# Both score passes as fp32r products of high and low parts, maxima turned on TensorE, elementwise work shared out anew

## The reference

```python
# _ref: q = layernorm(x) in 16 heads of 16, k = v = ctx
scores = jnp.einsum('bhqd,bhkd->bhqk', q, k) * scale
scores = jnp.where(causal_mask, scores, jnp.finfo(scores.dtype).min)
out = jnp.einsum('bhqk,bhkd->bhqd', jax.nn.softmax(scores, axis=-1), v)
# FFN
prob = jax.nn.softmax(xf @ w_router + b_router, axis=-1)
_, idx = jax.lax.top_k(prob, TOP_K)                 # mask: 1 for the 4 blocks in idx
h = jax.nn.relu(jnp.einsum('nd,ebd->neb', xf, w1b) + b1b[None])
y = jnp.einsum('neb,ebd,ne->nd', h, w2b, mask) + b2
# whole
x = x + jnp.tanh(g_xattn[0]) * xattn(layernorm(x), ctx, ctx)
x = x + jnp.tanh(g_ffn[0]) * ffn(layernorm(x), ...)
```

## Time and profile before

| | |
|---|---|
| time, median of 3 runs | 773.07 us (771.96 to 773.37) |
| profiled execution | 772.89 us, of which the span of the trace is 771.1 us |
| granted TensorE clock, mean | 0.987 of full |
| busy TensorE / its weight loads | 728.8 / 676.5 us (95% / 88%) |
| busy VectorE, ScalarE, GpSimd | 577.0, 432.7, 486.7 us |
| DMA, mean | 38 GB/s |

### The profile page before, as it was taken

One profiled execution on the slowest core, in us unless ns is written; L12 is line 12 of the kernel. 1 busy time (PEld: TensorE's weight loads), 2 busy tenths in 40 slices (PEclk: granted clock), 3 DMA queues, 4 the chain that ended last, 5 costly groups with the idle time before them and its releaser, 6 DMA issues. The chain is left out here.

```text
span 771.1 us, 26802 instructions
## 1 busy us (share of the span) xinstructions
PE 728.8 (95%) x11496; PEld 676.5 (88%) x11496; DVE 577.0 (75%) x1362; ACT 432.7 (56%) x780; POOL 486.7 (63%) x663
## 2 busy tenths in 40 slices
PE   4578899999999999999999999999999999999877
PEld 3457799999999999999999999999999999998877
DVE  5278787778778877787887778778777877877652
ACT  2266556655665565566556555655665566556432
POOL 5386566667666766676676667666766766665432
PEclk9599999999999999999999999999999999999999
DMA  6201111111011111101111110111111101000000
GB/s 161 67 31 31 29 45 34 40 44 32 29 43 45 43 30 44 44 16 44 43 44 30 44 43 20 41 44 44 41 33 45 35 25 43 17 16 2 16 28 28
DMA packets 30101, 29.65 MB, mean 38 GB/s; under 512 B 3745, under 2 KB 29473, under 8 KB 29985
## 3 DMA queue, kind: packets, MB, share of 16 engines
q1 hardware_dynamic: 29984, 27.95, 11.8%
HBM read 19.03 MB, written 8.39 MB: 36 GB/s over the span
## 5 line engine op out<-in xcount | busy, mean ns | idle before, releaser
L661 POOL TENSOR_SCALAR_AFFINE_SELECT weights<-weights 128x1024 f32<-128x1024 f32 x128 | 137.6, 1099 | 130.6 <-ACT weights L434 130.6
L668 POOL TENSOR_TENSOR h_low<-hid,h_high 128x512 fp32r<-128x512 f32 x128 | 166.1, 1297 | 56.2 <-ACT hid L456 55.3
L567 DVE SCALAR_TENSOR_TENSOR hid<-bank,b_cols,used_all 128x256 f32<-128x256 f32 x256 | 111.2, 475 | 72.2 <-PE bank L362 63.9
L360 PE MATMUL bank<-xT_high,w_high 128*128 128x256 f32 x512 | 154.7, 302 | 3.6 <-DVE hid L567 3.6
L514 DVE TENSOR_REDUCE q_pad<-score_banks 128x16 f32<-128x2048 f32 x64 | 146.0, 2282 | 9.5 <-PE score_banks L258 9.5
L434 ACT ACTIVATE weights<-score_banks 128x1024 f32<-128x1024 f32 x128 | 124.3, 1024 | 43.1 <-PE score_banks L274 43.1
L378 PE MATMUL bank<-w_high,h_high 128*128 128x256 f32 x512 | 143.7, 281 | 2.6 <-DVE y_out L552 2.6
L361 PE MATMUL bank<-xT_low,w_high 128*128 128x256 f32 x512 | 144.4, 282 | 0.0
L362 PE MATMUL bank<-xT_high,w_low 128*128 128x256 f32 x512 | 144.1, 282 | 0.0
L379 PE MATMUL bank<-w_low,h_high 128*128 128x256 f32 x512 | 143.0, 279 | 0.0
L380 PE MATMUL bank<-w_high,h_low 128*128 128x256 f32 x512 | 143.0, 279 | 0.0
(11 more groups left out here) (76 smaller groups left out, 1286.3 us busy)
## 6 DMA issues: line engine op xcount, KB each, us to landing
c_in<-in_ctx SPq DMA_DIRECT2D x32, 256.0 KB, 2.8
x_in<-in_x SPq DMA_DIRECT2D x32, 256.0 KB, 3.1
out_y<-y_out SPq DMA_DIRECT2D x32, 256.0 KB, 2.2
w_stage<-in_w1T SPq DMA_DIRECT2D x1, 1024.0 KB, 8.8
hid<-in_w2T SPq DMA_DIRECT2D x16, 64.0 KB
qT<-qT SPq DMA_DIRECT2D x64, 8.0 KB
b_cols<-in_b SPq DMA_DIRECT2D x16, 0.2 KB
b_all<-in_b SPq DMA_DIRECT2D x1, 128.0 KB, 4.1
```

The source lines that it names most:

```text
L360: pe.matmul(out=bank, lhsT=w1_high[:, k, c], rhs=high, start=k == 0, stop=False)
L567: dve.scalar_tensor_tensor(hid[:, n % 4, j], banks[HID_BANK][:, j * TOKS:(j + 1) * TOKS], b1_cols[:, c:c + 1], used_all[:, p % 2], ALU.add ...
L661: pool.affine_select(out=w, in_=w, compare_op=ALU.is_ge, fill=0.0, base=0, pattern=[[0, 2 * HB], [1, S]], channel_multiplier=-1).then_inc( ...
L668: pool.tensor_tensor(h_low[:, p % 2, chunks], hid[:, n % 4], h_high[:, p % 2, chunks].bitcast(F32), ALU.subtract).then_inc(h_low_made, 1)
```

## The change

- Queries and context are split in a high part, rounded to fp32r, and a low part. For the context both lie side by side in the 32 columns of a head (`c_parts`) before they are turned; for the queries each value stands twice (`qn`), and the split is made after the transpose: ScalarE's copy rounds (`qT_high`), VectorE subtracts (`queries_low`). A product of 32 rows then holds (q high or low) x (k high + k low). Both passes run over `qT_high` and `qT_low`.
- The maximum goes through `neg_max` in a high and a low part, is turned by TensorE by itself (`max_transposed`), copied by ScalarE (`max_evacuated`), and is added in the second pass by four more products per 128 columns with the constant `pick`. `max_row` and its 64 DMAs go, `MAX_LAG` goes.
- The sum of x and attention goes from VectorE to GpSimd, the gate is multiplied into the normalisation. The two reciprocal roots of a turn are made in one pair of instructions (`deviations`).
- Hidden units: ScalarE adds the bias and clips from PSUM, in four instructions of 256 a turn, VectorE masks from SBUF in two of 512, ScalarE rounds one turn later, GpSimd subtracts there.
- The router's subtraction and clipping are taken together, the causal mask of the first pass gets one column less per group and constants for it.

```diff
@@ sizes, tiles
-MAX_LAG = 2
+        pick = sb("pick", [P, HB, P], F32R)
+        qn = sb("qn", [P, 2, HEADS, 2, HD], F32)
+        c_parts = sb("c_parts", [P, 2, HEADS, 2, HD], F32)
-        qT = sb("qT", [P, TS, BANK], F32)
-        kT = sb("kT", [P, TS, BANK], F32)
+        qT_high = sb("qT_high", [P, TS, BANK], F32R)
+        qT_low = sb("qT_low", [P, TS, BANK], F32R)
+        kT = sb("kT", [P, TS, BANK], F32R)
+        neg_max = sb("neg_max", [P, 2, U, PAD], F32)
+        max_high = sb("max_high", [P, U, HB], F32R)
+        maxT = sb("maxT", [P, S], F32R)
@@ TensorE
+            def max_transposed(b):
+                pe.wait_ge(max_low_made, b + 1)
+                if b >= 2:
+                    pe.wait_ge(att_copied, b - 1)
+                else:
+                    pe.wait_ge(k_copied, b + 2)
+                pe.transpose(banks[M0][:, D:D + S], neg_max[:, b % 2].rearrange("p u c -> p (u c)"),
+                             ident[:]).then_inc(max_turned, 1)
             def scores(b):
...
                 for r in range(HB):
                     cols = slice(r * S, (r + 1) * S)
-                    for u in range(U):
-                        rows = slice(u * PAD, (u + 1) * PAD)
-                        pe.matmul(out=score_banks[:, u, cols], lhsT=qT[rows, s, cols], rhs=kT[rows, s, cols],
-                                  start=r == 0, stop=False, tile_position=(u * PAD, 0))
+                    for n, queries in enumerate((qT_high, qT_low)):
+                        for u in range(U):
+                            rows = slice(u * PAD, (u + 1) * PAD)
+                            pe.matmul(out=score_banks[:, u, cols], lhsT=queries[rows, s, cols], rhs=kT[rows, s, cols],
+                                      start=r + n == 0, stop=False, tile_position=(u * PAD, 0))
...
             def shifted_scores(b):
                 s = b % TS
-                pe.wait_ge(max_landed[s], 16 * (b // TS + 1))
+                pe.wait_ge(max_copied, b + 1)
...
                 for r in range(HB):
                     cols = slice(r * S, (r + 1) * S)
+                    for n, queries in enumerate((qT_high, qT_low)):
+                        for u in range(U):
+                            rows = slice(u * PAD, (u + 1) * PAD)
+                            pe.matmul(out=score_banks[:, u, cols], lhsT=kT[rows, s, cols], rhs=queries[rows, s, cols],
+                                      start=r + n == 0, stop=False, tile_position=(u * PAD, 0))
                     for u in range(U):
                         rows = slice(u * PAD, (u + 1) * PAD)
-                        made = pe.matmul(out=score_banks[:, u, cols], lhsT=kT[rows, s, cols], rhs=qT[rows, s, cols],
-                                         start=True, stop=True, tile_position=(u * PAD, 0))
+                        made = pe.matmul(out=score_banks[:, u, cols], lhsT=pick[rows, r], rhs=maxT[rows],
+                                         start=False, stop=r == HB - 1, tile_position=(u * PAD, 0))
...
                 if 0 <= i - 2 < N:
                     x_transposed(i - 2)
+                if 0 <= i + 1 < N:
+                    max_transposed(i + 1)
@@ ScalarE
+            def keys_high(b):
...
+                act.copy(c_parts[:, b % 2, :, 0, :].bitcast(F32R),
+                         c_in[:, b % CS, :].rearrange("p (h d) -> p h d", d=HD)).then_inc(c_high_made, 1)
+            def hidden_clipped(p, m):
...
+                for j in range(PC):
+                    c = PC * m + j
+                    act.activation(hid[:, n % 4, j], banks[HID_BANK][:, j * TOKS:(j + 1) * TOKS], ACT.Relu,
+                                   bias=b1_cols[:, c:c + 1]).then_inc(hid_clipped, 1)
@@ ScalarE, its loop
+                if lp is not None:
+                    hidden_high(lp, lm)
+                    hidden_high(lp, lm + 1)
+                if p is not None:
+                    hidden_clipped(p, m)
+                if 0 <= i + 3 < N:
+                    keys_high(i + 3)
...
                 if 0 <= i < N:
                     exponentials(i)
                 if p is not None:
-                    hidden_parts(p, m)
+                    hidden_clipped(p, m + 1)
+                if 0 <= i + 1 < N:
+                    max_evacuated(i + 1)
                 if 0 <= i - 2 < N:
                     x_copies(i - 2)
-                if p is not None:
-                    hidden_parts(p, m + 1)
@@ VectorE
+            def queries_low(b):
+                dve.wait_ge(q_high_made, b + 1)
+                dve.tensor_tensor(qT_low[:, b % TS, :], banks[M1][:], qT_high[:, b % TS, :].bitcast(F32),
+                                  ALU.subtract).then_inc(q_low_made, 1)
             def row_maximum(b):
                 dve.wait_ge(scored, b + 1)
...
+                high, low = (neg_max[:, b % 2, :, n * HB:(n + 1) * HB] for n in range(2))
+                dve.tensor_reduce(out=high, in_=score_banks[:].rearrange("p u (r k) -> p u r k", k=S),
                                   axis=AX_X, op=ALU.max, negate=True).then_inc(max_found, 1)
+                dve.tensor_copy(max_high[:], high).then_inc(max_high_made, 1)
+                dve.tensor_tensor(low, high, max_high[:].bitcast(F32), ALU.subtract).then_inc(max_low_made, 1)
...
+                dve.tensor_tensor(hid[:, n % 4], hid[:, n % 4], used_all[:, p % 2].unsqueeze(1).to_broadcast([P, PC, TOKS]),
+                                  ALU.mult).then_inc(hid_made, 1)
@@ VectorE, its loop
                 if 0 <= i - OUT_LAG - 1 < N:
                     finished(i - OUT_LAG - 1)
+                if 0 <= i - 2 < N:
+                    layernorm_stats_again(i - 2)
+                if 0 <= i + 2 < N:
+                    queries_low(i + 2)
                 if 0 <= i + 1 < N:
                     row_maximum(i + 1)
@@ GpSimd, its loop
             for i in ITERATIONS:
+                lp, lm = hidden_pair(i - 1)
                 if 0 <= i - 2 < N:
+                    attention_added(i - 2)
+                if -3 <= i < N + 2:
+                    deviations(i)
+                if 0 <= i - 2 < N:
+                    bias_added(i - 2)
                 if 0 <= i + 3 < N:
+                    keys_low(i + 3)
                     values(i + 3)
+                if lp is not None:
+                    hidden_low(lp, lm)
+                    hidden_low(lp, lm + 1)
                 if 0 <= i < N:
                     causal_weights(i)
-                if p is not None:
-                    hidden_low(p, m)
-                    hidden_low(p, m + 1)
@@ SyncE
-            def max_row(b):
-                s, ride = b % TS, b + MAX_LAG
-                sync.wait_ge(q_copied, ride + 1)
-                sync.dma_start(qT[MAX_COL::PAD, s, :], qT[RIDE_COL::PAD, ride % TS, :]).then_inc(max_landed[s], 16)
```

325 lines of the change are left out of this document (179 added, 146 removed).

## The result

The changed kernel takes 886.56 us (884.88 to 888.97) against 772.52 for the kernel before: a ratio of 1.1485, 95% interval 1.1445 to 1.1525. It is slower, as forecast, but by 114 us and not by 37, and the time lies far above the range of 738 to 836. The profiled execution spans 887.0 us.

The account below looks back on a forecast made before the run. TensorE's instruction sum bounds the kernel for some 600 us, other engines mattering only if late. Turns +34, start +2.5 and end +1 make +37.5 on the profiled 772.9: 810 us, own range 797 to 826, full range 738 to 836.

Parts of the forecast that it names:

- is each step still hidden?: Check of VectorE, ScalarE and GpSimd per turn: VectorE 9.2 us against a turn of 11.7, all steps hidden behind TensorE.
- slack 0.7 and 0.4 us: Room before TensorE asks: 0.7 us for VectorE's maximum before the second pass, 0.4 for GpSimd's low parts of hidden units.
- (3): Rival: another engine binds, maximum or hidden units' low parts late by 0.5 us a turn; 840 us, chance 0.10.
- (1): Rival: moving columns, not weight loads, space TensorE's fp32r products, 12 to 15 ns each; 744 us, chance 0.22.
- (2): Rival: row groups of fp32r overlap badly on TensorE, 59 ns per instruction; +177 us, 950 in all, chance 0.10.
- (4): Rival: TensorE still splits fp32r products in two instructions, 2.7 us a turn; its chance is counted within rival (2).
- The turn: One tile's loop on TensorE: +0.58 us for added score products and a transpose, in 59 turns +34 us.
- The two passes: Score passes on TensorE: 16 more instructions at 28.4 to 29.5 ns, 0.45 to 0.47 us, other 64 adding 0 to 0.07.
- the transpose: One added TensorE transpose of the maxima per turn, 0.10 us.
- The start: First loads, constants and turns 0 to 4: up to -7 for the queue, +1.5 and +8 against it; +2.5 us.
- four turns: Early turns without FFN, bound by a chain: 9.4 to 9.9 us for 7.6, some +2 each, +8 together.
- The end: Last tiles: a longer hidden-unit path +1, two turns of query transposes fewer -1 at most; together +1 us.

Follow-up runs that it names:

- a_hidden_old: Changed kernel with the hidden units' path of the kernel before: VectorE adds bias and masks from PSUM, low parts at a turn's end; 904.45 us.
- a_quiet: Changed kernel with GpSimd's low part of hidden units cut to 8 of 256 columns, causal select to 1 of 128; 811.17 us.
- a_low_first: Changed kernel with GpSimd's two low parts of the hidden units moved ahead of the bias sum, context's low part and values; 879.58 us.
- a_mask_psum: Changed kernel with VectorE adding bias and masking hidden units from PSUM, the low parts staying at their new place; 900.77 us.

## Why the prediction was wrong

**The step that failed** is "is each step still hidden?". It added up VectorE's turn to 9.2 us from durations of rows of the kernel before, where xn and xT_low (440 and 419 ns) stood beside a GpSimd that was idle or nearly so, and took them to be properties of the instructions. Beside GpSimd's reads the same two took 1276 and 1218, and the mask 1187 for the 650 reckoned: 762.9 us in all for 589. The change moved GpSimd's low parts from the end of a turn to its middle, beside xn and the mask; it took the mask's input from PSUM to SBUF, which makes it a form that can be held up; and it gave GpSimd two more steps that read. The order of the queues was read only for who comes late (slack 0.7 and 0.4 us), and neither is what came late: between 100 and 700 us TensorE waited once for the maximum (0.6 us), not for the low parts, but 30.3 us for the gating and 18.5 for the router's first step, which stand behind the held-up steps in VectorE's queue. The 1.0 us of 40 elements beside a select was the row to ask about.

**The rivals.** (3) had the right outcome, another engine becomes the bound, with a wrong mechanism and price (840, by lateness of 0.5 us a turn). The lateness it named exists, 94.6 us of it, but in a_hidden_old. Its chance of 0.10 was too low for a step that rested on durations of many instructions at places where the change was to move them. (1), (2) and (4) fell, as said.

**What held, and what only cancelled.** With GpSimd quiet the kernel takes 811.17 us, and 810 was forecast. That they agree so closely is luck, for most terms behind it did not hold. TensorE's timeline in a_quiet: the fifth, sixth and seventh causal masks (one set a turn), and two sets of products before the first of these; then the clock from 40 to 84 us in the changed kernel (columns as in the earlier trace rows):

```profile
61.13 0.45 PE L275 MATMUL score_banks<-kT,qT_low 32*128 32x128 f32 x4
61.34 0.45 PE L275 MATMUL score_banks<-kT,qT_high 32*128 32x128 f32 x4
...
61.77 0.69 PE L281 MATMUL score_banks<-tri,place 32*128 32x128 bf16 x16
...
74.67 0.69 PE L281 MATMUL score_banks<-tri,place 32*128 32x128 bf16 x16
...
84.70 0.43 PE L281 MATMUL score_banks<-tri,place 32*128 32x128 bf16 x16
...
40.00:84.00 44.00, 36.93 (x511) 31.81 (x510) 21.73 (x51) 18.66 (x35) 23.62 (x30) 0.54 0.08 26
```

- The turn. From the seventh mask to the last a_quiet takes (744.94 - 84.70) / 57 = 11.58 us a turn, and before 11.15: +0.43 and not +0.58, 24.7 us in 57 turns where 34 were reckoned for 59. The two passes take 2.44 us for 2.11, +0.33 and not +0.45 to 0.54 (28 ns a product, the low end and under), and the transpose 0.1 as reckoned.
- The start. The seventh masks stand at 84.70 and before at 64.69: +20.0 and not +2.5. (The extra fill of a_quiet is not the reason: the changed kernel has its seventh masks at 84.34.) Most of it comes from four turns: from the third masks to the seventh the kernel before takes 33.3 us, the changed kernel 50.5, which is +17.2 where +8 was reckoned. These turns were priced at +2 us each, from durations at the 2.4 GHz level; in a_quiet the turn that was to be 9.4 to 9.9 us long is 12.1, 12.3, 12.9 and 10.0. In the first three of these its sets of four products stand 0.21 us apart and last 0.45, where it is 0.11 and 0.28 later. The changed kernel, whose start is as long, shows a granted clock of 0.54 from 40 to 84 us, near the 1.2 GHz level. In a_quiet the profile's clock column says 1.00 there, so for that run the level is inferred from the durations alone. The kernel before has left the low level by 40.77 us, where a pass takes 1.17 us for the 2.09 of 25.34. TensorE was at work for 18.6 of the first 40 us in a_quiet, for 20.9 in the changed kernel and for 19.7 in the kernel before. Why the level stayed low in one kernel and rose in the other was not tested.
- The end. From the last masks to the end of the span: 64.6 us in a_quiet, 70.9 before: -6.3 and not +1. This too was not taken apart.

Together 24.7 + 20.0 - 6.3 = 38.4, on 771.1, where 37.5 was forecast: the start came out 17.5 us over its term, the turns and the end 9 and 7 under theirs. On top of it the changed kernel has 57 x (12.88 - 11.58) = 74 us in which VectorE is held up, and some 4 at the end.

## What to carry to other kernels

A duration of a VectorE instruction read from a trace holds for what GpSimd did beside it. Before pricing a move on either engine, mark each VectorE step that has two SBUF inputs or is a cast or a scalar product, and lay GpSimd's reading instructions beside it in the new order (for scalar products its fills, too). As far as these traces show, the price of a meeting is what is left of the GpSimd instruction, whatever the size of the VectorE step. An input in PSUM or a reduction frees a step, and a shorter GpSimd instruction makes the meeting cheaper. But count the other steps as well: in a_low_first, a_hidden_old and a_mask_psum the steps that were freed got faster, and others were held up or came late in their place. No run here kept all the work of the changed kernel and won the loss back. The sign that it happens already is a group whose mean is well above its quickest instruction, or a microsecond for 40 elements.

## What the runs showed of the hardware

- A cast of 16 elements took 1.05 us and a difference of 16 elements 1.20 beside two GpSimd instructions of 1.26 us, as long as steps of 256 elements (a scalar product 0.85, a difference 1.18 on average in the same run). In a_hidden_old, where GpSimd's long steps stand elsewhere, the two took 0.18 each on average.
- Taking half of the score instructions away made the kernel 2.3% slower (b_single), while VectorE's router steps and its sum of x and attention met GpSimd's reads.
- An fp32r product of 32 rows with 128 columns costs 28 ns in four row groups, one of the two fp32 instructions 28.4, and 64 moving columns instead of 128 save nothing.
- GpSimd's select took 1244 ns on average in the changed kernel and 1099 before. Whether VectorE holds it up in its turn was not tested.
